# A cross-attention loop's probability mix in three fp32r passes, with GpSimd splitting its operands

## The reference

```python
qx = _ln(qx, qxln_w, qxln_b)                       # queries of the 32 tokens
kvx = jnp.einsum('bsi,oi->bso', cond, w_kv_x)      # cond: the context, 512 rows
kx, vx = jnp.split(kvx, 2, axis=-1)
kx = _ln(kx.reshape(b, sc, g, d), kxln_w, kxln_b)
scores = jnp.einsum('bsghd,btgd->bghst', q, k) * scale
p = jax.nn.softmax(scores, axis=-1)
xout = jnp.einsum('bghst,btgd->bsghd', p, v)
```

## Time and profile before

| | |
|---|---|
| median of the runs shown | 428.82 us (428.65 to 429.05) |
| the profiled execution | 429.2 us, of it 427.0 us span |
| granted TensorE clock | 1.000, every slice |
| PE busy | 98% of the span |
| DVE busy | 81% |
| ACT busy | 58% |
| GpSimd busy | 9% |

### The profile page before, as it was taken

How to read it: one execution, slowest core, us unless ns; L and a number is a source line. 1 busy time by engine, 2 the same in 40 slices (tenths; PEclk the granted TensorE clock), 3 DMA queues, 4 the chain that set the end, 5 groups by cost and what they waited for, 6 DMA issues and landing times.

```text
span 427.0 us, 6939 instructions
## 1 busy us (share of the span) xinstructions
PE 417.7 (98%) x2459; PEld 295.8 (69%) x2465; DVE 347.0 (81%) x705; ACT 248.9 (58%) x780; POOL 37.4 (9%) x58
## 2 busy tenths in 40 slices
PE   7999999999999999999999999999999999999897
PEld 3453455788885767778676686785597799937586
DVE  5789999987999899689899998978986788446831
ACT  2478898788547777748986578564505263220220
POOL 0010000040000001101001000110201015001000
PEclk9999999999999999999999999999999999999999
DMA  7599120500002015993555835698566988530000
GB/s 230 224 188 413 44 93 2 198 2 22 30 2 98 1 51 123 220 295 72 128 124 101 196 70 100 156 205 338 101 121 211 390 297 220 104 123 2 2 2 26
DMA packets 14592, 56.82 MB, mean 133 GB/s; under 512 B 1824, under 2 KB 2912, under 8 KB 13280
## 3 DMA queue, kind: packets, MB, share of 16 engines
q1 hardware_dynamic: 11104, 39.31, 24.9%
q0 software_dynamic: 3456, 17.11, 21.3%
HBM read 41.40 MB, written 0.26 MB: 98 GB/s over the span
## 4 chain that ended last, share of the span: by engine, by line
PE 83%; DVE 9%; ACT 2%; DMA 2%; issue 1%; POOL 1%; SPq 0%; DVEq 0%; ACTq 0%
PE PS L479 11%; PE PS L1840 10%; PE PS L450 9%; PE PS L451 9%; PE PS L452 9%; PE PS L1869 3%; PE PS L1179 3%; PE PS L1313 3%; PE PS L530 3%; PE PS L1855 2%; PE PS L1161 2%; DMA raw_dt.float<-in_wk_nat 2%; PE PS L489 1%; PE PS L1164 1%; PE PS L1165 1%
## 5 line engine op out<-in xcount | busy, mean ns | idle before, releaser
L613 ACT ACTIVATE sq_dt.float<-PS 128x128 bf16<-128x128 f32 x256 | 67.0, 279 | 26.9 <-PE PS L452 20.4
L479 PE MATMUL PS<-s_dt.float,ctx_ring_dt.float 128*128 128x512 f32 x128 | 57.8, 593 | 0.0
L613 ACT ACTIVATION_READ_ACCUMULATOR sq_dt.float<-PS 128x1 f32 x256 | 53.6, 209 | 0.0
L450 PE MATMUL PS<-wkc_dt.float32r,ctx_hi_dt.float32r 128*128 128x512 f32 x128 | 51.5, 403 | 0.1
L451 PE MATMUL PS<-wkT_dt.float32r,ctx_hi_dt.float32r 128*128 128x512 f32 x128 | 50.0, 390 | 0.0
L452 PE MATMUL PS<-wkc_dt.float32r,ctxT_ring_dt.float32r 128*128 128x512 f32 x128 | 50.0, 390 | 0.0
L1840 PE MATMUL PS<-wch_dt.float,xs_dt.float 128*128 128x512 f32 x96 | 42.0, 592 | 0.0
L479 PEld LDWEIGHTS PS<-s_dt.float,ctx_ring_dt.float 128*128 128x128 f32 x128 | 23.6, 190 | 23.6 <-issue 23.0
L695 ACT ACTIVATE luttmp_dt.float<-low_bit_dt.float,vec_dt.float,small_dt.float 128x1536 f32<-128x1536 uint8 x24 | 38.5, 1654 | 2.0 <-DMA lutw_dt.float<-luttmp_dt.float 2.0
L708 POOL DMA_DIRECT2D lutw_dt.float<-luttmp_dt.float x21 | 18.4, 875 | 207.4 <-DVE luttmp_dt.float L702 207.4
L702 DVE SCALAR_TENSOR_TENSOR luttmp_dt.float<-idx_dt.float,luttmp_dt.float 128x1536 f32<-128x1536 uint8 x21 | 36.5, 1755 | 0.0
(11 more groups left out here) (312 smaller groups left out, 859.1 us busy)
## 6 DMA issues: line engine op xcount, KB each, us to landing
lutw_dt.float<-luttmp_dt.float POOLq DMA_DIRECT2D x21, 768.0 KB, 6.2
wch_dt.float<-in_chunks SPq DMA_DIRECT2D x5, 1024.0 KB, 7.9
ctxT_ring_dt.float<-in_ctxT SPq DMA_DIRECT2D x8, 512.0 KB, 3.3
ctx_ring_dt.float<-in_ctx SPq DMA_DIRECT2D x8, 512.0 KB, 3.4
keysT_dt.float<-in_ctxT SPq DMA_DIRECT2D x8, 512.0 KB, 7.2
keys_dt.float<-in_ctx SPq DMA_DIRECT2D x8, 512.0 KB, 8.0
zu_dt.float<-in_wproj SPq DMA_DIRECT2D x1, 2048.0 KB, 7.2
A_first_dt.float<-in_wproj SPq DMA_DIRECT2D x1, 2048.0 KB, 8.0
```

The source lines that it names most:

```text
L450: nc.tensor.matmul(o, x_hi, hi[:, c, :], start=c == 0, stop=False)
L479: last = nc.tensor.matmul(mix_bank(b, c), keysr[k][:, t, c * 128:c * 128 + 128], sS[k][:, t, :], start=t == 0, stop=t == KT - 1)
L613: last = nc.scalar.activation(sq[:, (4 * hf + g) * D:(4 * hf + g + 1) * D], key_bank(b, 2 * t + hf)[:, g * D:(g + 1) * D], ACT.Square, acc ...
```

## The change

For batches 1 to 6 the mix is made of three fp32r passes per k-tile instead of one fp32 matmul: high context by high probabilities, high context by low probabilities, low context by high probabilities. Batches 0 and 7 stay in fp32. GpSimd makes the parts: `split_keys` copies the batch's context rounded to fp32r and subtracts the copy from it in place; `high_part` and `low_part` do the same per k-tile with the probabilities; `add_tile` adds the tiles up for `total`, which DVE's `sums` did. The exponentials of batches 1 to 6 are four instructions of one k-tile, placed in two pairs before and after the squares of one tile of the next batch. `sums` on DVE remains for batches 0 and 7. `total` moves ahead of half 1 of the mix from step 2 on, and `spread` into the middle of that half. On ACT `leaf(b-1, 0)` moves to the head of the step; on DVE `term(b-1, 0)` moves from before `shift` to behind the split of the context; on GpSimd the DMA of part 0 is issued after the third k-tile and those of parts 1 and 2 at the end of the batch. Buffers: `p_hi` and `keys_hi` are new, single; the low parts replace their sources in place.

```diff
@@ def step (PE)
-                if prev and more:
+                if prev and more and isinstance(b, int) and b == 1:
                     mix(b - 1, 1 - k, 1)
                     total(b - 1)
                     spread(b)
+                elif prev and more:
+                    total(b - 1)
+                    mix(b - 1, 1 - k, 1, range(2))
+                    spread(b)
+                    mix(b - 1, 1 - k, 1, range(2, KT))
@@ def mix (PE)
+                whole = isinstance(b, int) and b in (0, B - 1)
                 if c == 0:
-                    pe.wait_ge(p_ready, b + 1)
-                    pe.wait_ge(ld_ctx[k], 8 * (b - k) + 16)
+                    if whole:
+                        pe.wait_ge(p_ready, 4 * b + 4)
+                        pe.wait_ge(ld_ctx[k], 8 * (b - k) + 16)
+                    else:
+                        pe.wait_ge(keys_split, b)
...
                 for t in tiles:
-                    last = nc.tensor.matmul(mix_bank(b, c), keysr[k][:, t, c * 128:c * 128 + 128], sS[k][:, t, :],
-                                            start=t == 0, stop=t == KT - 1)
+                    o, part = mix_bank(b, c), slice(c * 128, c * 128 + 128)
+                    if whole:
+                        last = nc.tensor.matmul(o, keysr[k][:, t, part], sS[k][:, t, :], start=t == 0, stop=t == KT - 1)
+                    else:
+                        if c == 0:
+                            pe.wait_ge(p_split, 4 * b + t - 3)
+                        nc.tensor.matmul(o, keys_hi[:, t, part], p_hi[:, t, :], start=t == 0, stop=False)
+                        nc.tensor.matmul(o, keys_hi[:, t, part], p_lo[k][:, t, :], start=False, stop=False)
+                        last = nc.tensor.matmul(o, keys_lo[k][:, t, part], p_hi[:, t, :], start=False, stop=t == KT - 1)
@@ def step (ACT)
+                if b > 1:
+                    leaf(act, b - 1, 0)
                 if more:
                     split_A(act, b + 1)
                 if b:
-                    for m in range(3):
+                    for m in range(1 if b > 1 else 0, 3):
                         leaf(act, b - 1, m)
...
+                if more and b:
+                    if b == 1:
+                        squares(b + 1, 1 - k, 0)
+                    exponentials(b, k, range(2))
+                    squares(b + 1, 1 - k, 1 if b == 1 else 0)
+                    exponentials(b, k, range(2, KT))
+                    for t in range(2 if b == 1 else 1, KT):
                         squares(b + 1, 1 - k, t)
                     key_rstd(b + 1, 1 - k)
...
@@ def loop_pool (GpSimd)
-            for k in range(1, LUT_STEPS):
-                add_terms(pool, k)
+            def split_keys(b, k):
+                pool.wait_ge(ld_ctx[k], 8 * (b - k) + 16)
+                if b > 1:
+                    pool.wait_ge(pctx, 2 * b)
+                nc.gpsimd.tensor_copy(keys_hi, keysr[k]).then_inc(keys_hi_ready, 1)
+                pool.wait_ge(keys_hi_ready, b)
+                nc.gpsimd.tensor_tensor(keys_lo[k], keysr[k], keys_hi, ALU.subtract).then_inc(keys_split, 1)
+            def high_part(b, k, t):
+                pool.wait_ge(p_ready, 4 * b + t + 1)
+                self_step(nc.gpsimd.tensor_copy(p_hi[:, t, :], sS[k][:, t, :]))
+            def low_part(b, k, t):
+                nc.gpsimd.tensor_tensor(p_lo[k][:, t, :], sS[k][:, t, :], p_hi[:, t, :], ALU.subtract).then_inc(p_split, 1)
+            def add_tile(b, k, t):
+                total = nc.gpsimd.tensor_tensor(ps, sS[k][:, 0, :] if t == 1 else ps, sS[k][:, t, :], ALU.add)
...
+            for b in range(1, B - 1):
+                k = b % 2
+                split_keys(b, k)
...
+                high_part(b, k, 0)
+                high_part(b, k, 1)
+                pool.wait_ge(sum_full, b)
+                add_tile(b, k, 1)
+                low_part(b, k, 0)
+                low_part(b, k, 1)
+                for t in range(2, KT):
+                    high_part(b, k, t)
+                    add_tile(b, k, t)
+                    low_part(b, k, t)
+                    if b > 1 and t == 2:
+                        add_terms(pool, b - 1, range(1))
+                if b > 1:
+                    add_terms(pool, b - 1, range(1, 3))
@@ def step (DVE)
                 if b > 1:
                     lo_of_A(dve, b + 1)
-                sums(b - 1, 1 - k)
+                else:
+                    sums(0, 0)
                 maxima(b)
                 if b == 1:
                     lo_of_A(dve, 2)
-                term(dve, b - 1, 0)
+                    term(dve, 0, 0)
                 shift(b, k)
...
                 if b == 4:
                     split_weights()
+                if b > 1:
+                    term(dve, b - 1, 0)
                 term(dve, b - 1, 1)
```

More of the change, by code:

```diff
@@ L68 @@
     ("s", 2 * KT * NK, LOOP, LAST, "wch"), ("catx", NH * T, LOOP, LAST, "zu"),
-    ("px", CT * NH * 64, LOOP, LAST, "catc"), ("qtmp", 1280, LOOP, LAST, "catc"),
-    ("vecs", 5 * NK, LOOP, LAST, "raw"), ("ctx_hi1", CT * NK, LOOP, LAST, "raw"),
+    ("px", CT * NH * 64, LOOP, LAST, "catc"), ("qtmp", 768, LOOP, LAST, "catc"),
+    ("p_hi", KT * NK, LOOP, LAST, "qtmp"),
+    ("vecs", 4 * NK, LOOP, LAST, "p_hi"), ("ctx_hi1", CT * NK, LOOP, LAST, "vecs"),
     ("keys", B * KT * C, TAIL, LATE, "catc"),
@@ L241, in build @@
             "st_full", "scaled", "sum_read", "mxf_ready", "tr_full", "m_ready", "mb_full"))
+        p_split, keys_hi_ready, keys_split = sem("p_split"), sem("keys_hi_ready"), sem("keys_split")
         shifted, p_ready, psum_ready, sum_full, r_ready, pctx, px_ready = (sem(n) for n in (
@@ L335, in build @@
         mx, nm, R = buf("vecs", 512), buf("vecs", 512, skip=512), buf("vecs", 512, skip=1024)
-        ps2 = buf("vecs", 2, 512, skip=1536)
+        ps, ps_pair = buf("vecs", 512, skip=1536), buf("p_hi", 2, 512)
+        p_hi = buf("p_hi", KT, NK, dtype=fp32r)
+        p_lo = [buf("s", KT, NK, skip=k * KT * NK, dtype=fp32r) for k in range(2)]
+        keys_hi = buf("qfront", KT, C, dtype=fp32r)
+        keys_lo = [buf("ctx_ring", KT, C, skip=k * KT * C, dtype=fp32r) for k in range(2)]
         px = buf("px", CT, NH, 64)
@@ L488, in total @@
                 pe.wait_ge(scaled, 4 * KT * 2 - 1 if isinstance(b, int) and b == B - 1 else 4 * b + 7)
-                nc.tensor.matmul(bank(2), ones, ps2[:, 0, :], start=True, stop=True).then_inc(sum_full, 1)
+                nc.tensor.matmul(bank(2), ones, ps, start=True, stop=True).then_inc(sum_full, 1)
             def project_core(parts):
@@ L637, in step, with exponentials @@
                     split_context(b + 2, k)
-                if more:
-                    for t in range(1 if b == 0 else 0, KT):
+                if more and b:
[5 more added lines that the diff above has]
+                    for t in range(2 if b == 1 else 1, KT):
                         squares(b + 1, 1 - k, t)
                     key_rstd(b + 1, 1 - k)
-                exponentials(b, k)
+                elif more:
+                    for t in range(1, KT):
+                        squares(b + 1, 1 - k, t)
+                    key_rstd(b + 1, 1 - k)
+                if not (more and b):
+                    act.wait_ge(shifted, b + 1)
+                    nc.scalar.activation(sS[k], sS[k], ACT.Exp, scale=SCALE).then_inc(p_ready, KT)
                 if prev and not more:
                     inverse(b - 1)
-            def exponentials(b, k):
+            def exponentials(b, k, tiles):
                 act.wait_ge(shifted, b + 1)
-                nc.scalar.activation(sS[k], sS[k], ACT.Exp, scale=SCALE).then_inc(p_ready, 1)
+                for t in tiles:
+                    nc.scalar.activation(sS[k][:, t, :], sS[k][:, t, :], ACT.Exp, scale=SCALE).then_inc(p_ready, 1)
             def inverse(b):
@@ L703, in term, with add_terms @@
                                            lutt[:, m, :], ALU.is_equal, ALU.mult).then_inc(lut_term, 1)
-        def add_terms(pool, k):
-            for m in range(3):
+        def add_terms(pool, k, parts=range(3)):
+            for m in parts:
                 pool.wait_ge(lut_term, 3 * k + m + 1)
@@ L717, in loop_pool @@
                 nc.gpsimd.tensor_copy(wpc_hi[:, 4 * i:4 * i + 4, :], wpc[:, 4 * i:4 * i + 4, :]).then_inc(wpc_hi_ready, 1)
-            for k in range(1, LUT_STEPS):
-                add_terms(pool, k)
+            def split_keys(b, k):
[12 more added lines that the diff above has]
+                total = nc.gpsimd.tensor_tensor(ps, sS[k][:, 0, :] if t == 1 else ps, sS[k][:, t, :], ALU.add)
+                if t == KT - 1:
+                    total.then_inc(psum_ready, 1)
+                    pool.wait_ge(psum_ready, b + 1)
+                else:
+                    self_step(total)
+            pool.wait_ge(catc_ready, 4)
+            pool.wait_ge(beta_turned, 1)
+            for b in range(1, B - 1):
+                k = b % 2
+                split_keys(b, k)
+                if b == 1:
```

(13 more changed lines are left out.)

2 lines of the change are left out of this document (1 added, 1 removed).

## The result

The changed kernel takes 492.35 us (median of 4 runs, 491.42 to 493.00) against 428.74 for the kernel before on the same chip: 1.148 times, 95% interval 1.147 to 1.150. It is slower, as forecast, but by 63.6 us where 12.8 were forecast, and the time lies outside the range of 422 to 453. In the rows PE is TensorE, DVE VectorE, ACT ScalarE and POOL GpSimd.

The account below looks back on a forecast made before the run. PE bounds the kernel before; after the change DVE does: 116.5 work + 27.5 waiting for GpSimd + 5.1 other waits = 149.1 us in steps 2 to 6, 12.7 more, so 429.2 + 12.7 + 0.05 = 442.0, median 441.6; range 422 to 453.

Parts of the forecast that it names:

- PE's term: Mix of batches 1 to 5 in three passes saves 6.75 us over steps 2 to 6, leaving 129.7 if PE stays dense.
- rival 1: PE stays the bound, DVE waiting under 1.6 us a batch: stretch 129.7, end 422.1 us; chance 0.22.
- The sign: Whole kernel: slower, at chance 0.70, with DVE as the bound and the stretch of steps 2 to 6 growing by 12.7 us.
- scaled tiles: In each step PE would wait for DVE's scaled score tiles and for the maxima; no size for each wait.
- I take 5.5, nearer the upper end: DVE's waiting for GpSimd in each batch, taken between 3.2 and 6.4 us; five batches of steps 2 to 6: 27.5 us.
- the upper price: GpSimd's two-input operations at 2.5 times a copy: 14.8 us a batch; all borne by DVE, 7.6 a batch, end 452.
- GpSimd's time: Thirteen GpSimd instructions hold it 12.5 us a batch, between 7.8 and 14.8, with two-input operations at twice a copy.
- Who is held: Only DVE groups with two SBUF inputs lock against GpSimd: 59.7 us of steps 2 to 6, 51% of 116.5.
- by chance: GpSimd's 12.5 us a batch falls by chance on DVE's work, so 6.4 us a batch must be pulled apart.
- rival 3: Lookup table's DMA lands late at the leaf: some 2 us in steps 3 to 6, 8 us added, 449.6; chance 0.08.
- The sums off VectorE: Sums leaving DVE save some 1.86 us a batch, 9.3 us over steps 2 to 6, leaving DVE 116.5 us of work.
- The new order of ScalarE and VectorE: Edits around the mix, such as moved exponentials and terms, cost together about 0; exponentials in step 1 cost 1.4 us.

Follow-up runs that it names:

- experiment 1: The changed kernel without the loop's fifteen accumulating transfers of the table, leaf waiting for the term before it instead: 465.42 us, ratio 1.083.
- experiment 2: The changed kernel with GpSimd's thirteen operations a batch on one column, mix on fixed tiles: 427.30 us; also without transfers: 421.54 us, its rows set beside experiment 1.
- experiment 7: The kernel before, with the mix in three passes on fixed tiles: 423.23 us; separately with VectorE's sums on one column: 428.55 us.
- experiment 5: The changed kernel without the loop's accumulating transfers, and GpSimd's three additions a batch on one column: 451.70 us, 13.7 us less than experiment 1.

## Why the prediction was wrong

**Right.** PE's term: the stretch without interference was 129.82 us (129.7 forecast), and rival 1's 422.1 stands beside 421.54. The passes come 0.23 us apart at the full clock (last section). The sign, and the reason for it (VectorE held by GpSimd becomes the bound), hold: work that nobody waits for makes 33.9 us of 43.9. In experiment 1 PE waits for VectorE in the scores of each of steps 3 to 7, 3.8 to 11.0 us a step; the forecast named scaled tiles, and in three of the five it is, in whole or in part, the reading of the values.

**The step that failed first: "I take 5.5, nearer the upper end".** It measured 44.4 / 5 = 8.9 us a batch in the stretch, beyond the 6.4 that the forecast held possible at its price for GpSimd, and the 7.6 at the upper price. Two causes show in the rows, the second the larger:
- GpSimd's time. Undisturbed, the subtraction of 512 takes 1.26 to 1.28 us (estimate 1.04), that of 1024 2.36 (2.08), a cast of 512 0.61 (0.52). The batch then holds it for 1.04 + 2.36 + 4 x 0.61 + 7 x 1.27 = 14.7 us, not 12.5.
- Who is held. The forecast took operations with two SBUF inputs alone, and left some of them out. The groups that it counted gained 30.0 of the 44.4 us, by the rows of experiment 2's two kernels, not far from its 27.5. The other 14.3 fell on what it hadn't counted: 9.8 on `tensor_scalar`s with one SBUF input (8.4 in the quantisation, 1.4 in `key_scale`, where one goes from 179 to 469 ns), 4.5 on two-input operations of `key_scale` and a bf16 addition of the quantisation. The Trainium skill's page "SBUF — State Buffer", section "Who interferes with whom", has it so: besides operations with two SBUF inputs, `tensor_scalar` in its fast two-port modes takes the shared pair, and an operation with at most one SBUF input outside those modes doesn't. The trace agrees: 681 ns for L970, which reads PSUM and a small SBUF operand (684 before).

Whether "by chance" failed as well isn't shown. With the groups left out, 73.4 us of VectorE's 116.5 can be held; by chance 14.7 us of GpSimd then meet 9.3 a batch (an estimate from these numbers), and 8.9 was measured. Group by group it is uneven: the end of `normalise`, which comes when GpSimd starts on a batch, gained 9.6 us, the five `lo_of_A` splits none.

**The second: rival 3, at 8 us and 0.08.** Its mechanism is there (68.1 us of waits at `leaf`), its price was 26.9 us. The forecast took 2 us late in each of four steps; the waits are up to 11.7 us. By the rows of step 3, the terms' delay by VectorE's lengthening, the issue behind the last split and a longer landing add up, and the later leaves, which the forecast left out, wait as well as the first and hold up the inverse. The landing was not GpSimd's own doing: with its work on one column it was still 14.5 us at most. In the trace the long landings stand beside SyncE's loads (87.8% of the DMA engines' time from 188 to 195 us), of which the forecast said only that SP's queue is as before. The forecast also kept the two mechanisms apart: without GpSimd's work the transfers cost 5.8 us, with it 26.9.

**The sum.** From 441.6: 16.9 for the lengthening (44.4 less 27.5), 4.4 for VectorE's waits and gaps (170.43 less 156.44 is 14.0 in experiment 1; the forecast's 149.1 left 9.6 beside 139.5 of busy time), 2.6 outside the stretch (it begins at 153.22, not 150.73), 26.9 for the transfers: 492.4, against 492.35. Each term is a difference between runs, so that the sum has to close; it shows the sizes and proves nothing.

**Smaller.** The sums off VectorE were counted at 9.3 us, but only on VectorE's side, where they belonged while it was the bound; experiment 7 shows they were worth nothing as long as PE is, and experiment 5 that GpSimd asks more for them. The new order of ScalarE and VectorE is not free as long as the transfers are there: 427.30 us with GpSimd's work on one column, against 423.23 for the passes alone in the old order, though the sums are off VectorE. Without the transfers it is 421.54.

## What to carry to other kernels

Before moving elementwise work to GpSimd, list VectorE's operations that run in the same phase: here those with two SBUF inputs and `tensor_scalar`s on SBUF waited out GpSimd's instructions, those with a PSUM operand didn't, and the lengthening was paid almost in full, whether or not anyone waited for GpSimd's result. An engine that issues transfers between computations makes them late by what stands ahead of them in its queue; look for the consumer that stands at the head of another engine's step, and move that consumer rather than hope for the transfer. Price moved work by what it costs at its new place: the sums took 1.86 us a batch where they were free and 2.3 where they were not.

## What the runs showed of the hardware beyond that

GpSimd waits as VectorE does. In the kernel with one-column work, three terms of VectorE run back to back, and each 128x1 operation of GpSimd lasts as long as a term:

```profile
165.50 5.09 DVE L741 SCALAR_TENSOR_TENSOR luttmp_dt.float<-idx_dt.float,luttmp_dt.float 128x1536 f32<-128x1536 uint8 x3
...
167.38 1.60 POOL L776 TENSOR_TENSOR vecs_dt.float<-vecs_dt.float,s_dt.float 128x1 f32<-128x1 f32 x1
169.05 1.59 POOL L772 TENSOR_TENSOR p_hi_dt.float32r<-s_dt.float,p_hi_dt.float32r 128x1 fp32r<-128x1 f32 x1
...
170.84 0.19 POOL L776 TENSOR_TENSOR vecs_dt.float<-vecs_dt.float,s_dt.float 128x1 f32<-128x1 f32 x1
```

1.60 us beside the terms, 0.19 behind them; VectorE's terms stay at 1.70 each. So the two take turns by whole instructions. A short one on GpSimd costs VectorE little; a long one that comes first can cost it most of its length: in experiment 2's last timeline 1.9 us (2.60 in place of 0.69) for one of 2.36.

TensorE came back slow from waits of some 4 us. The timeline of PE in step 3 of experiment 1, after a wait of 4.00 us for a scaled tile:

```profile
182.92 0.80 PE L461 MATMUL PS<-A_hi_dt.float32r,ctx_hi_dt.float32r 128*128 128x512 f32 x1 [4.00 <-DVE s_dt.float L826]
...
183.94 0.63 PE L463 MATMUL PS<-A_hi_dt.float32r,ctxT_ring_dt.float32r 128*128 128x512 f32 x1
184.37 0.63 PE L461 MATMUL PS<-A_hi_dt.float32r,ctx_hi_dt.float32r 128*128 128x512 f32 x1
...
188.41 0.39 PE L501 MATMUL PS<-s_dt.float32r,qfront_dt.float32r 128*128 128x512 f32 x1
188.64 0.39 PE L502 MATMUL PS<-p_hi_dt.float32r,ctx_ring_dt.float32r 128*128 128x512 f32 x1
```

Up to 188.2 us the passes start 0.43 us apart, from there 0.23. The granted clock is 0.50 (1.2 GHz) between 183 and 188 us, 1.00 (2.4 GHz) between 189 and 194. Over steps 2 to 6 of the changed kernel its mean is 0.87.
